# First mixture and the front of the state-space part in one phase, with the mixture's blocks ordered by chunk

## The reference, cut to what matters

```python
x = x + attention(layernorm(x))
# first mixture: of 8 experts, each token goes to its two best
logits = tokens @ router_w.T
topv, topi = top_k(logits, 2); w = softmax(topv)
out = sum over e of gate[:, e] * (gelu(tokens @ w1[e].T) @ w2[e].T)     # hidden 256
x = x + out
# state space: rms norm, input product, causal convolution of 4 taps, scan
h = rmsnorm(layernorm(x)) * norm_w
u = h @ Win + b_in                    # 256 channels
u = conv4(u) + conv_b
hc = hc @ A[d] + u_t * Bm[d]; y = hc . Cm[d]     # for each channel d, 16 states, over 1024 steps
x = x + y @ Wout + b_out + layernorm(x)
x = x + second_mixture(layernorm(x))
```

## Time and profile before

| | us |
|---|---|
| median of 3 runs | 1007.68 |
| lowest and highest run | 1005.82, 1008.59 |
| span of the profiled execution, first to last instruction | 1006.1 |

### The profile page before, as it was taken

The page is one execution under the profiler, slowest core; times in us unless marked ns, Lnnn a source line. Parts: engine busy times, 40 slices in busy tenths (PEclk is TensorE's granted clock), DMA queues, the critical chain, the costliest instruction groups (busy, mean ns, idle before and its releaser), DMA issues. The chain is left out here.

```text
span 1006.1 us, 25740 instructions
## 1 busy us (share of the span) xinstructions
PE 860.1 (85%) x9276; PEld 721.8 (72%) x9276; DVE 554.6 (55%) x1617; ACT 449.2 (45%) x957; POOL 474.5 (47%) x501
## 2 busy tenths in 40 slices
PE   4999999999998518989567789999967999999990
PEld 1777777777776516877555579999966679999990
DVE  4666666676576534656359776455467713222225
ACT  5545455354453104555146757333504444444443
POOL 3235353343444463777666100126422376767764
PEclk9999999999999757999779999999998999999995
DMA  7676800000000013333330010000023023322245
GB/s 237 236 283 260 332 21 11 13 16 5 21 10 14 22 43 86 109 103 99 80 96 2 3 24 2 3 4 1 1 80 133 24 70 83 86 85 90 82 116 167
DMA packets 72920, 79.31 MB, mean 79 GB/s; under 512 B 14429, under 2 KB 56676, under 8 KB 72320
## 3 DMA queue, kind: packets, MB, share of 16 engines
q1 hardware_dynamic: 61744, 59.69, 18.8%
q0 software_dynamic: 9216, 16.84, 4.9%
q10 hardware_dynamic: 1872, 1.58, 0.5%
HBM read 32.46 MB, written 47.77 MB: 80 GB/s over the span
## 5 line engine op out<-in xcount | busy, mean ns | idle before, releaser
L436 POOL TENSOR_TENSOR attn_qd<-attn_qT,attn_qpow 128x512 f32<-128x512 f32 x32 | 51.3, 1604 | 129.9 <-DVE attn_qT L727 129.9
L1466 ACT ACTIVATE routed_hT<-routed_hid,routed_B 128x256 f32<-128x256 f32 x160 | 65.7, 470 | 81.1 <-PE routed_hid L1389 81.1
L1035 POOL DMA_INDIRECT mixed<-moe_outs,moe_target x80 | 77.7, 972 | 39.2 <-DVE moe_outs L1137 16.7
L1307 POOL DMA_INDIRECT results<-routed_outs,routed_target x80 | 78.5, 981 | 30.0 <-issue 16.3
L1292 POOL DMA_INDIRECT queue_in<-routed_XN,routed_slot x64 | 63.1, 985 | 46.4 <-DVE routed_slot L1567 22.2
L1401 PE MATMUL routed_outp<-routed_W,routed_hT 128*128 128x128 f32 x640 | 77.8, 275 | 0.0
L1389 PE MATMUL routed_hid<-routed_cols,routed_W 128*128 128x256 f32 x320 | 75.8, 380 | 0.5 <-DVE routed_cols L1615 0.5
L1401 PEld LDWEIGHTS routed_outp<-routed_W,routed_hT 128*128 128x128 f32 x640 | 74.7, 192 | 0.1
L426 POOL DMA_INDIRECT sorted_rows<-attn_sent_rows,attn_slot x56 | 57.1, 1019 | 18.3 <-issue 14.1
L1389 PEld LDWEIGHTS routed_hid<-routed_cols,routed_W 128*128 128x128 f32 x320 | 57.8, 191 | 6.8 <-ACT routed_shared L1445 0.7
L307 ACT ACTIVATE attn_kd<-attn_turn,attn_kpow 128x256 f32<-128x256 f32 x56 | 23.5, 470 | 77.3 <-PE attn_turn L585 77.3
(11 more groups left out here) (332 smaller groups left out, 2270.6 us busy)
## 6 DMA issues: line engine op xcount, KB each, us to landing
sorted_rows<-attn_vacant SPq DMA_DIRECT2D x8, 2080.0 KB, 8.7
moe_rows<-sorted_rows SPq DMA_DIRECT2D x44, 130.0 KB
queue_in<-attn_empty SPq DMA_DIRECT2D x8, 645.0 KB, 6.6
routed_rows<-queue_in SPq DMA_DIRECT2D x40, 129.0 KB, 2.3
results<-attn_zero SPq DMA_DIRECT2D x8, 512.0 KB, 8.1
ssm_turn_buf<-mixed SPq DMA_DIRECT2D x16, 256.0 KB, 3.7
routed_W<-m1w SPq DMA_DIRECT2D x2, 2048.0 KB, 10.2
xs<-x SPq DMA_DIRECT2D x8, 256.0 KB, 4.4
```

The source lines that it names most:

```text
L436: pool.tensor_tensor(wide(of_pair(qd, p)), wide(of_pair(qT, p)), qpow[:, p * P:(p + 1) * P].unsqueeze(1).to_broadcast([P, BATCH, P]), ALU. ...
L1035: pool.indirect_dma_start(results, bass.IndirectOffsetOnAxis(target[:, n:n + 1], 0), outs[q][:, j * P:(j + 1) * P], None, bounds_check=2 * ...
L1307: pool.indirect_dma_start(results, bass.IndirectOffsetOnAxis(target[:, n:n + 1], 0), outs[t % KEPT_BACK][:, j * P:(j + 1) * P], None, boun ...
L1466: last = act.activation(hT[t % 2][:, m * GROUP:(m + 1) * GROUP], banks[q % 4][:, (m % 2) * GROUP:(m % 2 + 1) * GROUP], ACT.Silu, bias=B1[: ...
```

## The change

The two phases become one (`mixed_space_phase`), written out without loops over blocks.

- The table orders blocks by chunk and then by expert: a block belongs to the chunk in which it is begun, so that after `complete(c)` blocks all of chunk c is done (11 for the first chunk, 4 more for each further one). There are 39 blocks.
- The work stands in 53 ticks. Tick t has block t on every engine. Ticks 0 to 19 carry two sets of squares each, one ahead of the block on PE and one behind it. The squares have one bank on either side, and both copies are ACT's.
- Each chunk's front stands at fixed ticks, 4 apart: POOL's add in tick 15 + 4c, DVE's add and its moments in 16, scaled means and tokens in 17, transposes in 18, products in 19 and 20, taps from 20 to 24. The add of the second half goes from POOL to DVE. Transposed rows have one bank instead of two, and a chunk's transposes and products share one.

The order of blocks, the ticks' numbers and SP's fetch of a chunk's results:

```diff
+BLOCKS = (2 * BATCH * SEQ + EXPERTS * (GROUP - 1)) // GROUP
+def complete(c):
+    return (2 * WIDE * (c + 1) + EXPERTS * (GROUP - 1)) // GROUP
...
+            blocks_of(slice(0, LAST))
             logits_read(LAST, proj[1])
...
+        PERIOD = complete(1) - complete(0)
+        NSQUARES = LEVELS * NT
+        def due(t, begin):
+            c, part = divmod(t - begin, PERIOD)
             return c if part == 0 and 0 <= c < CHUNKS else None
+        FETCHED_BACK, MIXED, STATED, SCALED, TURNED, INPUT, KEPT_IN, CONVOLVED = 18, 15, 16, 17, 18, 19, 20, 22
+        TICKS = CONVOLVED + 2 + PERIOD * (CHUNKS - 1) + 1
...
+            def fetch_back(c):
+                sp.wait_ge(s["sent"], BODY + complete(c))
```

POOL's ticks:

```diff
+            for t in range(TICKS):
+                if t < BLOCKS:
+                    sent_back(t)
+                if 2 <= t < BLOCKS + 2:
+                    landed(t - 2)
...
+                if due(t, STATED) is not None:
+                    deviations(due(t, STATED))
+                if due(t, MIXED) is not None:
+                    mixed(due(t, MIXED))
```

PE's set of squares and its ticks:

```diff
+            def squares(m):
+                k, q = divmod(m, NT)
+                n = 2 ** k
+                if m:
+                    pe.wait_ge(s["lev_b"], m)
+                    pe.wait_ge(s["lev_c"], m)
+                for left, right, bank in ((c3, b3, squares_b), (b3, c3, squares_c)):
...
+            for t in range(TICKS):
+                if 2 * t < NSQUARES:
+                    squares(2 * t)
+                if t + 2 < BLOCKS:
+                    rows_turned(t + 2)
+                if t + 1 < BLOCKS:
+                    hidden_of(t + 1)
+                if t < BLOCKS:
+                    output_of(t)
+                if due(t, INPUT + 1) is not None:
+                    input_product(due(t, INPUT + 1), 1)
+                if due(t, INPUT) is not None:
+                    input_product(due(t, INPUT), 0)
+                if due(t, TURNED) is not None:
+                    columns(due(t, TURNED))
+                if 2 * t < NSQUARES:
+                    squares(2 * t + 1)
```

ACT's ticks:

```diff
+            for t in range(TICKS):
+                if t < BLOCKS:
+                    gelu_of(t)
+                if 1 <= t <= NSQUARES // 2:
+                    power_kept(2 * t - 1)
+                if t + 2 < BLOCKS:
+                    first_weights(t + 2)
+                if due(t, INPUT) is not None:
+                    columns(due(t, INPUT))
+                for h in range(2):
+                    if due(t, KEPT_IN + h) is not None:
+                        channels(due(t, KEPT_IN + h), h)
+                        last_tap(due(t, KEPT_IN + h), h)
+                if due(t, SCALED) is not None:
+                    tokens(due(t, SCALED), 0)
+                    tokens(due(t, SCALED), 1)
+                if t < NSQUARES // 2:
+                    power_kept(2 * t)
```

DVE's ticks:

```diff
+            for t in range(TICKS):
+                if t + 2 < BLOCKS:
+                    columns_of(t + 2)
+                if t < BLOCKS:
+                    kept_of(t)
+                if t + 2 < BLOCKS:
+                    second_weights(t + 2)
+                if due(t, STATED) is not None:
+                    mixed(due(t, STATED))
+                    stated(due(t, STATED))
+                if due(t, SCALED) is not None:
+                    scaled_means(due(t, SCALED))
+                for n in range(TAPS - 1):
+                    if due(t, CONVOLVED + n) is not None:
+                        convolved(due(t, CONVOLVED + n), n)
```

More of the change, by code:

```diff
@@ L1801, in _, with fetch @@
         def _(sp):
-            for c in range(CHUNKS):
+            def fetch(n):
+                first = sp.value_load(table.first_row[n:n + 1, 0:1], min_val=0, max_val=EXPERTS * REGION)
+                sp.wait_ge(s["rows_read"], n + 1)
+                sp.dma_start(by_row(rows[n % BODY]), sorted_rows[bass.ds(first, GROUP), :].rearrange("(p j) f -> p j f", p=P)
+                             ).then_inc(fetched[n % BODY], 16)
+            def fetch_back(c):
+                sp.wait_ge(s["sent"], BODY + complete(c))
                 if c >= 2:
@@ L1806, in _ @@
                     sp.dma_start(wide(back[k][:, c * WIDE:(c + 1) * WIDE]), result_view[:, k, c]).then_inc(back_in[c % 2], 16)
+            for n in range(TICKS):
+                if n < BLOCKS:
+                    fetch(n)
+                if due(n, FETCHED_BACK) is not None:
+                    fetch_back(due(n, FETCHED_BACK))
             sp.wait_ge(s["g_out"], 2)
@@ L1827, in mixed @@
                 chunk = slice(c * WIDE, (c + 1) * WIDE)
-                for k in range(2):
-                    if k:
-                        pool.wait_ge(s["added"], 2 * c + 1)
-                    pool.tensor_tensor(xs[:, chunk], xs[:, chunk], back[k][:, chunk], ALU.add).then_inc(s["added"], 1)
+                pool.tensor_tensor(xs[:, chunk], xs[:, chunk], back[0][:, chunk], ALU.add).then_inc(s["added"], 1)
             def deviations(c):
@@ new lines, in _, with rows_turned, hidden_of @@
+            pe.sem_inc(s["outp"], 2)
+            def rows_turned(n):
+                pe.wait_ge(fetched[n % BODY], 16 * (n // BODY + 1))
+                pe.wait_ge(s["cols"], n + 2)
+                for j in range(2):
+                    mm = pe.transpose(turn[:, j * P:(j + 1) * P], rows[n % BODY][:, j * TAGGED:j * TAGGED + D], ident[:, :])
+                mm.then_inc(s["turned"], 1)
+            def hidden_of(n):
+                pe.wait_ge(s["w1_in"], n + 1)
+                pe.wait_ge(s["cols"], n + 3)
+                pe.wait_ge(s["act"], n + 1)
+                for m in range(HB):
+                    mm = pe.matmul(hid[n % 2][:, m * GROUP:(m + 1) * GROUP], w1[n % 2][:, m * P:(m + 1) * P], cols[n % 2],
+                                   start=True, stop=True)
+                mm.then_inc(s["hid"], 1)
@@ new lines, in output_of @@
+            def output_of(n):
+                pe.wait_ge(s["act"], n + 3)
+                pe.wait_ge(s["w2_in"], n + 1)
+                pe.wait_ge(s["outs"], n + 1)
+                for j in range(2):
+                    for m in range(HB):
+                        mm = pe.matmul(outp[n % 2][:, j * P:(j + 1) * P], acts[n % 2][:, m * GROUP + j * P:m * GROUP + (j + 1) * P],
+                                       w2[n % 2][:, m * P:(m + 1) * P], start=(m == 0), stop=(m == HB - 1))
+                mm.then_inc(s["outp"], 1)
@@ L2228, in _ @@
[L2228 to L2241 removed]
+            dve.sem_inc(s["cols"], 2)
@@ new lines, in mixed @@
+            def mixed(c):
+                chunk = slice(c * WIDE, (c + 1) * WIDE)
+                dve.wait_ge(s["added"], 2 * c + 1)
+                dve.tensor_tensor(xs[:, chunk], xs[:, chunk], back[1][:, chunk], ALU.add).then_inc(s["added"], 1)
+            second_weights(0)
+            second_weights(1)
+            columns_of(0)
+            columns_of(1)
+            dve.wait_ge(s["zeroed"], 2)
+            for t in range(TICKS):
[13 more added lines that the diff above has]
+                        convolved(due(t, CONVOLVED + n), n)
```

434 lines of the change are left out of this document (159 added, 275 removed).

## The result

The changed kernel takes 1038.4 us (median of four runs, 1035.8 to 1039.8), the kernel before 1006.8 beside it: 1.0315 times, 95% interval 1.0294 to 1.0335. That is 3% slower, as forecast in sign; the forecast was 1029.7 us for a run and its range (1008 to 1041) holds the time. The profiled execution is the fastest of the four, with a span of 1034.0 us (before 1006.1).

The account below looks back on a forecast made before the run. POOL paces the mixture; PE and DVE share the front's bound. Ticks, rounds and end put the windows at 615.4 us instead of 593.4, 22 us later: span 1028.1, run 1029.7 us, range 1008 to 1041.

Parts of the forecast that it names:

- The stretch: First hidden product of the mixture to first turned state-space window: 209 us before, windows forecast 22 us later.
- four rounds: Ticks 20 to 35, four ticks and one chunk per round: 17.6 + 3 x 19.0 = 74.6 us.
- What bounds it: Ticks 0 to 19: PE and ACT wait for each other over the squares' copies; 4.95 us at first, 5.5 at fifth level.
- The rival of ticks at PE's own 4.0 us: Ticks 0 to 19: copies hidden, 20 us back, forecast 1009; chance inside no change's 0.09 and the forecast's lower tail.
- Tick 17: ACT's copy of set 34 queues behind chunk 0's token scalings, which wait for DVE: set 35 starts 4.5 us later.
- The ring: Ticks 20 to 35: waits through POOL, DVE, ACT and PE queues close a loop, 18.2 us a round, 19.0 with lower clock.
- The first round: First four ticks from tick 20: lacks the last tap of an earlier chunk, so 17.6 us.
- The rule on the clock: PE in the rounds: bursts with waits between them start at the lower clock each time, 0.8 us a round.
- The end: Fifth round to first turned window: last scatter, fetch, add, moments, powers, tokens, products, taps; 43.4 us.
- POOL's pace: Rounds: means come before ACT reaches the tokens, no ring, 14.2 us a round, 1004; chance 0.10.
- The lower clock throughout: After tick 20 PE stays at its lower clock and is the bound, 1042; chance 0.11 with other slower cases.
- Attention and table at nothing: Wider block table and chunk counting hidden beside POOL's scatters and DVE's wait: 0; uncovered about 1 and 2 us.

Follow-up runs that it names:

- e4: Changed kernel with the squares' products going around three PSUM banks instead of two for sets 0 to 35: 1021.5 us.
- e1: Changed kernel with ACT's four token scalings moved to the next tick, behind its Gelu and copy, transposes and products one tick later: 1016.6 us.
- e3: Changed kernel with tokens behind the next tick's Gelu and the convolution taps in the three ticks that hold no moments: 1010.3 us.
- e11: Changed kernel plus unread PE products: three behind the outputs of ticks 20, 24, 28, 32, one ahead of those of ticks 22, 26, 30, 34: 1031.6 us.
- e7: Changed kernel plus three unread 128 x 512 PE products behind the block's outputs in ticks 20, 24, 28 and 32: 1038.0 us.
- e5: Changed kernel with tokens behind the next Gelu, taps in ticks without moments and three banks for the sets, joined: 995.5 us.

## Why the prediction was right, point by point

The stretch by the forecast's own steps, in us of the profiled execution:

| step | forecast | measured | places in the trace |
|---|---|---|---|
| first hidden product to tick 1 | 7.3 | 7.05 | 380.7, 387.76 |
| ticks 1 to 15 | 75.8 | 79.2 | 466.9 |
| ticks 16 to 18, with the hold-up | 21.4 | 23.9 | 490.9 |
| to the end of POOL's add of chunk 1 | 8.8 | 8.6 | 499.45 |
| four rounds | 74.6 | 75.8 | 575.24 |
| to the last scatter's end | 13.7 | 14.0 | 589.24 |
| to the first turned window | 29.7 | 30.6 | 619.83 |
| sum | 231.3 | 239.1 | |

- *What bounds it.* The ticks are bound by the copies, as said: e4 freed one bank's wait and they went from 5.21 to 4.38 us. The term was too small by 0.23 us a tick: behind a set, the block starts after 1.11 us and not 0.93, the block takes 2.12, and the fourth level's ticks are 5.4. The rival of ticks at PE's own 4.0 us did not come by itself; e4's third bank brought them to 4.38.
- *Tick 17.* The mechanism is the one forecast, and e1 removed it. Its size, 4.5, was 4.8; what the forecast left out is the clock behind it: tick 18 took 7.7 us instead of 5.9, its first set at 1.33; in e1, without the hold-up, it takes 5.7.
- *The ring.* Shown by e1 to e3: moving tokens and taps, with no work taken out, made the rounds 15.1 us. The steps agree to 0.7 us, but for a reason that was half wrong. The forecast gave 18.2 at the upper clock and 0.8 to the lower; e11 shows 17.2 and 1.4. The two errors cancel in part. The first round was wrong the other way: forecast shorter, 17.6, because a pair of taps is missing in it, it took 19.9. The lower clock lies later in it (granted 0.50 from 507.6 to 513), so that the hidden products and outputs behind the tokens' block take 1.91 and 1.70 us there, 1.34 and 1.05 in the second round; at the upper clock, in e11, the first round is 17.8. So the four rounds agree to 1.2 us because +2.3 in the first stands against -1.1 in the other three; that is luck.
- *The rule on the clock.* The Trainium skill, "TensorE: Matmul & The Clock Gate", section "HAM oscillation", by which bursts with waits between them start each time at the lower clock, is borne out for these outputs: 2.07 us behind a wait of 1.93 in e7, 1.16 in e11 where a useless product stands in it. It doesn't hold for every wait: e3's transposes behind 2.79 us took 0.41 us at a granted clock of 1.00 (timeline, PE):

```profile
527.95 0.41 PE L1792 MATMUL ssm_pb<-powers_ident,ssm_H 128*128 128x128 f32 x2 [2.79 <-DVE ssm_H L2208]
```

- *The end.* 44.6 us instead of 43.4, in the forecast's order: last scatter, fetch, add, moments, powers, tokens, products at the lower clock. But the forecast's addition slipped: from ACT's 29 us its steps sum to 42.35, not 43.4. With the right sum it is 1028.7 us for a run, and the end was 2.2 us too short: 1.9 because ACT was at chunk 6's taps until 30.9 us and not 29 (the tokens start at 606.11, counted from 575.24), the rest behind the tokens.
- *POOL's pace*, the rival on the other side, named its condition rightly: it decides once the tokens do not hold the ring. e3 met it, and came to 14.6 to 15.4 us a round, 1010 us; the forecast's figure for that case, 1004, lacked the ticks' excess and some 0.9 us a round. *The lower clock throughout* did not come: rounds with PE's clock at 0.8 on average were not 21 us long.
- *Attention and table at nothing.* The table's work lies beside the scatters, as forecast; their last now ends at 372.8, and the rows are turned 4.9 us after it (before 6.3, 375.3 to 381.6). It was not tried apart.

The miss of 8.7 us for a run, inside the range, is 7.8 us of the stretch, of which the ticks are 3.4, the clock behind tick 17 about 2, and the rounds and the end 2.4 (3.5 with the end's sum put right); the rest, 0.9, is less than the windows' slower start.

The gain that the overlap should have brought is thus not lost to work but to order and to a bank: 14 us to one bank too few for the squares, 6.7 to the tokens ahead of a copy, some 19 to tokens and taps in the ring of the rounds and in the two chunks behind them, the lower clock that their waits bring included. e5 takes these back and has the gain: 11.6 us less than the kernel before, on the same chip.

## What to carry to other kernels

When two phases are merged into fixed ticks, follow each wait to what stands behind it in the same queue: a step that waits for another engine must stand behind the work that others need, even if it gets later itself. A ring through four queues with no engine much over 75% busy is found by counting one round from one row back to itself, and it is shortened by order, not by taking work away. Count what a second, independent stream needs in banks as well as in time.
